# A two-layer perceiver on one core: a third pair of PSUM banks in the last blocks, projections moved between stages, root tables fetched ahead, first loads on a second queue, and products that nothing reads

## The reference

```python
x = x + L0_xattn(ln(x), ctx, mask)   # 16 heads of 16: softmax(q k^T / 4 + (1 - mask) * -10000) v
x = x + L0_attn(ln(x), ...)          # layernorm, causal linear attention over 128 rows, GELU feed-forward
x = x + L0_ffn(ln(x), ...)           # ternary weights, 8-bit activations, silu(gate) * up, down
x = x + L1_xattn(ln(x), ctx)         # as L0, no mask, output projection Wo
x = x + L1_attn(ln(x), ...)          # RWKV recurrence, as scans
x = x + L1_ffn(ln(x), ...)           # ternary w1, depthwise convolution of width 3, silu, ternary w2
```

## Time and profile before

| what | value |
|---|---|
| median of 3 runs | 1111.94 us (1110.3 to 1113.24) |
| the profiled execution | 1110.35 us |
| its span in the trace | 1108.6 us |
| TensorE matmul busy | 1010.3 us, 91% |
| VectorE busy | 737.9 us, 67% |
| ScalarE busy | 685.2 us, 62% |
| GpSimd busy | 437.5 us, 39% |
| mean granted TensorE clock | 0.953 |

### The profile page before, as it was taken

The page is one execution under the profiler, slowest core; times in us unless marked ns, Lnnn a source line. Parts: engine busy times, 40 slices in busy tenths (PEclk is TensorE's granted clock), DMA queues, the critical chain, the costliest instruction groups (busy, mean ns, idle before and its releaser), DMA issues. The chain is left out here.

```text
span 1108.6 us, 30442 instructions
## 1 busy us (share of the span) xinstructions
PE 1010.3 (91%) x12740; PEld 667.8 (60%) x12741; DVE 737.9 (67%) x1723; ACT 685.2 (62%) x963; POOL 437.5 (39%) x388
## 2 busy tenths in 40 slices
PE   7899999999999999887777899999999999999642
PEld 4466666666666666554532566666666666666421
DVE  4888888888888888833357656555656555555455
ACT  3677778777877877776431455555655565655622
POOL 4368888888888888773000000000000000000000
PEclk9999999999999999999985899999999999999965
DMA  7420112110122201130040000111110111000000
GB/s 300 135 69 19 53 66 68 68 56 31 52 69 68 68 22 49 51 151 7 4 180 1 2 24 13 35 35 35 35 35 2 35 35 35 2 2 2 2 1 5
DMA packets 14680, 53.29 MB, mean 48 GB/s; under 512 B 3024, under 2 KB 4816, under 8 KB 13648
## 3 DMA queue, kind: packets, MB, share of 16 engines
q1 hardware_dynamic: 14544, 51.35, 13.3%
HBM read 51.21 MB, written 0.13 MB: 46 GB/s over the span
## 5 line engine op out<-in xcount | busy, mean ns | idle before, releaser
L704 DVE TENSOR_REDUCE tile_max<-ps_max 128x1 f32<-128x448 f32 x448 | 261.0, 620 | 170.4 <-PE ps_max L992 168.1
L701 DVE CUSTOM_DVE_ANT_0 unread<-ps_max,masks 128x448 bf16<-128x448 f32 x432 | 253.6, 621 | 79.0 <-PE ps_max L992 65.6
L393 POOL TENSOR_TENSOR probs<-probs,masks 128x512 f32<-128x512 f32 x196 | 245.3, 1273 | 84.8 <-ACT probs L500 83.7
L509 ACT ACTIVATE probs<-ps_scores 128x1024 f32<-128x1024 f32 x196 | 190.0, 1021 | 96.6 <-PE ps_scores L1015 96.6
L504 ACT ACTIVATE probs<-probs 128x1024 f32<-128x1024 f32 x196 | 207.4, 1058 | 53.3 <-DVE probs L752 46.5
L1015 PE MATMUL ps_scores<-q_pad,k_full 32*128 32x256 f32 x3136 | 233.2, 380 | 0.0
L1031 PE MATMUL ps_out<-probs,values 128*32 128x128 f32 x6272 | 215.9, 278 | 6.1 <-ACT probs L504 5.8
L992 PE MATMUL ps_max<-k_high,q_high 32*128 32x448 bf16 x880 | 199.2, 367 | 17.1 <-DVE tile_max L704 10.1
L1031 PEld LDWEIGHTS ps_out<-probs,values 128*32 128x32 f32 x6272 | 160.5, 110 | 60.7 <-issue 51.1
L1015 PEld LDWEIGHTS ps_scores<-q_pad,k_full 32*128 32x128 f32 x3136 | 193.7, 187 | 0.9
L982 PE MATMUL ps_proj<-ctx_t,wk 128*128 128x448 f32 x368 | 161.8, 562 | 0.0
(11 more groups left out here) (232 smaller groups left out, 678.4 us busy)
## 6 DMA issues: line engine op xcount, KB each, us to landing
ctx_t<-in_ctx_t SPq DMA_DIRECT2D x28, 896.0 KB, 5.3
masks<-in_mask_n SPq DMA_DIRECT2D x14, 448.0 KB, 3.4
masks<-in_mask_t SPq DMA_DIRECT2D x14, 448.0 KB, 3.6
room_w<-in_L_attn_f_w SPq DMA_DIRECT2D x2, 1024.0 KB, 8.8
room_w<-in_L_ffn_w SPq DMA_DIRECT2D x2, 1024.0 KB, 7.5
room_w<-in_L_ffn_w_gate SPq DMA_DIRECT2D x1, 1024.0 KB, 10.6
room_w<-in_L_ffn_w_up SPq DMA_DIRECT2D x1, 1024.0 KB, 13.1
room_w<-in_L_ffn_w_down SPq DMA_DIRECT2D x1, 1024.0 KB, 15.1
```

The costliest lines, as they stand in the source:

```text
L393: nc.gpsimd.tensor_tensor(p, p, three(mask_t[m % 2], TILES)[:, t, :].unsqueeze(1).to_broadcast([P, 4, P]), ALU.add).then_inc(sig("bias_add ...
L509: nc.scalar.activation(prob(T, half), scores_half(half), ACT.Exp).then_inc(sig(f"exp_done{half}"), 1)
L701: ins = v.tensor_tensor_reduce(unread[:, j % 2, :], max_bank(m, j)[:, 0:HALF], mask_n[m % 2][:, HALF * half:HALF * (half + 1)], 1.0, -3e38 ...
L704: ins = v.tensor_reduce(tile_max[:, h, half:half + 1], ps_max[:, j % 2, 0:HALF], AX_X, ALU.max)
```

## The change

- Start: x, `wq` and `bq` of layer 0 are issued from ScalarE's queue; SyncE's begins with `wk`. TensorE computes 5 products of the identity with itself before x is there and 1 behind the first turn, into `ps_out`, which nothing reads. The maxima of block 0 use the `ps_scores` banks first and wait for `q_pad` only from the third on. GpSimd makes `max_change(0)` ahead of the cast `high(1, 1)`.
- Blocks 13 and 27: in odd tiles the first half of the scores goes to `ps_max`. Scores wait for the second half of the tile before and for the first half of two tiles before only. In block 13 VectorE adds the mask to both halves (`bias_last`), second half first, GpSimd adds none, and ScalarE only takes exponentials. No values are made in block 13.
- `BETWEEN` has 15 units: values of 14 take the place of values of 15, and the last key unit of 16 is gone from it. That unit and the values of 15 (`BESIDE`) go between the first maxima of layer 1. These maxima are now taken by pairs of halves, one VectorE instruction over two banks, in three pairs of banks.
- `root_table`: a square root of ones, on ScalarE, behind the last `sums_out` of layer 0 and behind the last GELU; the `between_out` units that stood ahead of `ln_root(1)` and `ln_root(4)` now follow them.
- Tail: 55 products of the identity with `wq[0]` (128x256 each) into `ps_out`, unread: 3, 4, 4, 18, 7, 11 and 8 at seven places.

```diff
@@ helpers
+        def is_last(m):
+            return m % NB == NB - 1
+        def scores_in(T, half):
+            if is_last(T // TILES) and T % TILES % 2 and half == 0:
+                return ps_max[:, :, :]
+            return ps_scores[:, 2 * half:2 * half + 2, :]
+        def pair_bank(i):
+            return (ps_scores[:, 0:2, :], ps_scores[:, 2:4, :], ps_max[:, :, :])[i % 3]
-        BETWEEN += [("v", NB + 1, u) for u in range(PAIRS)] + [("k", NB + 2, j) for j in range(4)]
+        BETWEEN += [("v", NB, u) for u in range(PAIRS)] + [("k", NB + 2, j) for j in range(3)]
+        BESIDE = [("k", NB + 2, 3)] + [("v", NB + 1, u) for u in range(PAIRS)]
+        BESIDE_AT = (1, 4, 7, 10, 13)
-            return m < BLOCKS and m != NB + 1
+            return m < BLOCKS and m not in (NB, NB + 1)
@@ sync
-            sp.dma_start(xs[0][:, :], a["x"]).then_inc(sig("x_loaded"), 16)
-            load_q_weights(0)
@@ gpsimd
-            for c in range(DC):
-                high(1, c)
+            high(1, 0)
...
+                if m == 0:
+                    high(1, 1)
                 for t in range(TILES):
-                    if l == 0:
+                    if l == 0 and not is_last(m):
                         add_bias(m, t)
@@ scalar
+            act.dma_start(xs[0][:, :], a["x"]).then_inc(sig("x_loaded"), 16)
+            act.dma_start(wq[0][:, :, :], a["L0_xattn_Wq"]).then_inc(sig("q_weights0"), 16)
+            act.dma_start(bq[0][:, :], ...).then_inc(sig("q_weights0"), 16)
+            def root_table():
+                act.wait_ge(sig("ones_set"), 1)
+                nc.scalar.activation(stat[:, 30:31], ones[:, 0:1], ACT.Sqrt).then_inc(sig("table_loaded"), 1)
...
-                        if l == 0:
+                        if l == 0 and is_last(m):
+                            exp_in_place(T, 1)
+                            exp_in_place(T, 0)
+                            lent_out(m, t)
+                            projected(m, t)
+                        elif l == 0:
...
-                            exp_scores(T, 0)
-                            exp_scores(T, 1)
+                            exp_scores(T, int(is_last(m)))
+                            exp_scores(T, 1 - int(is_last(m)))
...
-                    between_out(0)
+                    root_table()
                     ln_root(1)
-                    between_out(1)
+                    between_out(0, 1)
...
-                    between_out(8)
+                    act.wait_ge(sig("table_loaded"), 1)
+                    root_table()
                     ln_root(4)
-                    between_out(9)
+                    between_out(8, 9)
@@ vector
+            def pair_maximum(m, i):
...
+                dve.wait_ge(sig("max_ready"), 2 * H * m + 2 * i + 2)
+                two = pair_bank(i)
+                v.tensor_reduce(tile_max[:, i, :], two[:, :, 0:HALF], AX_X, ALU.max).then_inc(sig("max_free"), 2)
+            def bias_last(m, t):
+                T = TILES * m + t
+                dve.wait_ge(sig("bias_t"), 2 * m + 2)
+                need("pv_done", T - 1)
+                for half in (1, 0):
+                    dve.wait_ge(sig("scores_ready"), 2 * T + 1 + half)
+                    v.tensor_tensor(prob(T, half)..., scores_in(T, half)..., mask_t..., ALU.add).then_inc(sig("last_biased"), 1)
@@ tensor
+            def pair_maximum(m, h):
...
+                need("max_free", 2 * H * m + 2 * (h - 2))
+                for half in range(2):
+                    mm(pair_bank(h)[:, half, 0:HALF], ...).then_inc(sig("max_ready"), 1)
@@ tensor, scores
+                spare = is_last(m) and t > 0
+                if m < NB and spare:
+                    pe.wait_ge(sig("max_free"), 2 * H * NB)
+                    pe.wait_ge(sig("last_biased"), 2 * t - 1)
...
-                    pe.wait_ge(sig("exp_done0"), T)
+                elif m > NB or t > 0:
+                    pe.wait_ge(sig("exp_done0"), T - int(spare))
                     pe.wait_ge(sig("exp_done1"), T)
@@ tensor, the rest
+            def idle_products(n):
+                for _ in range(n):
+                    mm(ps_out[:, 0:D], ident[:, :], wq[0][:, 0, :], start=True, stop=True)
             pe.wait_ge(sig("idents"), 3)
+            for _ in range(5):
+                mm(ps_out[:, 0:P], ident[:, :], ident[:, :], start=True, stop=True)
...
+                    for i in range(H):
+                        pair_maximum(NB, i)
+                        if i in BESIDE_AT:
+                            beside_in(BESIDE_AT.index(i))
...
+            idle_products(3)
             pe.wait_ge(sig("ov_ready"), 1)
...
+            idle_products(18)
             pe.wait_ge(sig("wkv_ready"), 1)
```

96 lines of the change are left out of this document (72 added, 24 removed).

## The result

The changed kernel took 1096.19 us (median of 4, 1094.12 to 1096.39) beside 1111.61 of the kernel before in the same job (median of 4): ratio 0.9856, 95% interval 0.9838 to 0.9874. It is faster, but by 1.4% where 2.4% was forecast, and it lies above the range. The profiled execution took 1096.39, its span is 1094.7; before, 1108.6. So 13.9 us of span are to be found, where the forecast had 25.8.

A forecast was written before the change was run, and what follows sets the result against it. TensorE was taken as busy 91% of the span, waiting at the start, block 13, between the layers, block 27 and the tail. Terms summed to 25.8 us off 1110.35, 1084.6; it said 1085, range 1076 to 1094.

The forecast's parts named there:

- Start: Up to the first maxima: full clock earlier, context sooner, GpSimd reordered; −2.5 us, bounds +1 and −4.3.
- the clock comes up during the first key unit: Start: the 6 unread products raise TensorE's clock during that unit, not ahead of it; −2.0 us.
- the 0.4 taken for the three issues less ahead of the context: Start: three issues less on SyncE are about 1.3 us; 0.4 taken, the DMA engines being busy 0.93.
- the start gives nothing: Rival, start: context no earlier, x, wq and bq later by up to 1 us; 1087.5 us, chance 0.15.
- the change leaves blocks 0 to 12 and 14 to 26 as they are: First paragraph: these blocks stay unchanged but for their surroundings; forecast 0 for blocks 0 and 12.
- Block 13: Layer 0's last block: loop S, mask, mask, exponential, W takes 3.1 to 3.2 us per tile; −5.7, bounds −3.5 and −11.4.
- Between the layers: First root −0.5 us; fourth layernorm's root starts at 546.95 and the clock stays up, −3.7, bounds −2.4 and −3.7.
- First maxima of layer 1: Maxima by pairs take 17.4 us and start earlier, −4.2; less 1.7 for VectorE's waits: −2.5, bounds −1 and −4.2.
- Block 14: First tiles: clock falls after the last pair of maxima, returns one tile earlier; −2.0 us, bounds 0 and −7.3.
- Block 27: Last block: spare banks give 2.4 us per tile from tile 3, behind the late sums; −2.9, bounds −2 and −6.
- tiles 3 to 5 give 3 × 0.95: Block 27: each of these three tiles, behind the wait for the late sums, saves 0.95 us.
- Tail: Behind block 27: 55 unread products hold full clock and delay nobody; −6.0 us, bounds −3.5 and −6.0.

The follow-up runs named there:

- loads_back: The change with x, wq and bq issued from SyncE's queue again, ahead of wk: 1091.24 us, ratio 0.9809.
- bq_pause_filled: The change with 7 unread products instead of 1 behind the first turn, in the pause for bq: 1093.53 us, ratio 0.9815.
- start_filled: loads_and_block0 with unread products around layer 1's first maxima and in other pauses, plus 6 ahead of the first key unit: 1078.93 us, ratio 0.9721.
- block0_products: The change with 4 more unread products in the two pauses ahead of the first scores: 1092.04 us, ratio 0.9817.
- bq_back: The change with bq alone issued from SyncE's queue, ahead of wk: ratio 0.983; its profiled execution, 1434.57 us, is left out as slow.
- loads_and_block0: The change with x, wq, bq on SyncE's queue, 4 products ahead of the first scores, late sums' product at block 27's fifth tile: 1085.10 us, ratio 0.9743.
- no_tail_products: The change without the 55 unread products of the tail: 1100.65 us, ratio 0.9878.
- late_at_4: The change with the ones product of the late weights' sums at block 27's fifth tile instead of the third: 1092.39 us, ratio 0.9816.

## Why the prediction was wrong

It gave 1085 and 1076 to 1094; the result is 1096.2. (Its own sum gives 1084.6 for the profiled execution and so 1086.2 for the median; the 1.6 was dropped.) By its own steps:

**Start (−2.5; measured +0.5).** Failed: "the clock comes up during the first key unit", −2.0, and the 0.4 taken for the three issues less ahead of the context, which landed 0.1 to 0.2 earlier. The first maxima started at 19.55, 18.94 before, not "before 17". The products do lift the clock (loads_back), but a pause of 2 us for a load behind them keeps it down; with the pause filled the key unit runs at full clock (bq_pause_filled, start_filled). The rival *the start gives nothing* was right in its mechanism, loads landing later among `wk` and the context, and too mild in its size: it had up to 1 us later, q's projection is 3.2 later (9.11 for the 5.87 of before). The Trainium skill (DMA: Bandwidth & Descriptors, Issuing engines are not separate DMA queues) says that a second issuing engine saves the sequencer's time only. By that rule the start stands still, and the trace goes further: x, first on ScalarE's queue, was there 1.4 us later than as the first on SyncE's, and `bq` took twice as long to land.

**Block 0 (0; +4.0) and block 12 (0; +1.7).** The step that failed is the first paragraph's "the change leaves blocks 0 to 12 and 14 to 26 as they are". The order is unchanged, and a clock that falls in a place where the work has pauses of 1.1 us is not: the two stages were put at nothing without a reason that speaks of their pauses, and the earlier trace rows could not show them, since a fall of 3.4 us in a slice of 27.7 still prints a 9. block0_products shows it for block 0. Block 12 had one fall before too. It has the three pauses of 1.2 us in all 15 profiles (bq_back's left out), and 14 of them have one or two falls there, each 0.5 to 2.1 us behind the end of one of these pauses; the one without a fall, loads_and_block0, needs 33.07, with one fall 34.5 to 34.7, with two 36.1 to 36.2. Blocks 1 to 11 and 15 to 25 have no pause over 0.6 and no fall in any of them. Filling block 12's pauses was not tried, and why the clock falls behind one of them and not behind the next stays open.

**Block 13 (−5.7; −5.9).** Right, and by the loop it gave, S, mask, mask, exponential, W: 3.1 a tile forecast, 3.0 measured from 496.18 to 508.13. Undoing it gives 5.2 back. That the total meets so closely is partly luck: the last scores came 0.9 earlier than walked through, and a fall of the clock at 512.4, behind a pause of 2.08, gave it back (the last `weigh` 1.94 for 1.08; 25.7 in profiles without that fall).

**Between the layers (−0.5 and −3.7; −4.1 by the last down projection).** Right. The root stands at 546.74 where 546.95 was forecast (block 13 ends at 515.0 in either trace, the blocks ahead having lost what it gained, so the two can be compared), and the gate products run at full clock. The load is followed by its root 0.01 later again; the drain of the Trainium skill's page ScalarE: Activation LUTs (What ACT_TABLE_LOAD costs) was not seen.

**First maxima of layer 1 (−2.5; +0.1).** The mechanism was right, a unit at half clock makes VectorE wait once or twice; the term was mis-sized: 1.7 was put for the waits, 4.8 came (2.12 + 2.66). The reductions themselves took 16.5 instead of 17.4, and the first one started 0.5 later than forecast, counted from the down projection. At full clock the same instructions give the forecast and more: in the profile of no_tail_products, with nothing added there, the waits of over 1 us are gone and the way from the end of block 13 to the first scores is 4.8 shorter.

**Block 14 (−2.0; −3.6).** The mechanism was right, the pause after the last pair does bring the clock down again; filling it gives 3.8 more. Two tiles ran at half clock, four before, where the forecast had three.

**Block 27 (−2.9; −1.5).** The pace of the tiles was right, 2.52 for 2.4. What failed is "tiles 3 to 5 give 3 × 0.95": they gave 1.3, since the clock fell at 1031.2, behind the 1.90 of wait for the late sums, and the first two of them took 3.18 and 3.12. Without the wait the block gains 4.7 (late_at_4).

**Tail (−6.0; −5.1).** Right that the products hold the clock and delay nobody: without them 56.3 again. The turns stayed at half clock, behind a wait of 2.02 that the products leave there; the forecast had counted 0.5 for them, which is half of what is missing; the rest is 0.1 or so in each of four other steps. It was not tried with more products.

So the joined change was told right where computing was moved, and wrong where a load was moved and where only the clock moved. Of the 11.9 us that are missing 3.0 are the start, 5.7 are falls of the clock in blocks 0 and 12, 1.1 the stretch between the layers with block 14, 1.4 block 27 and 0.9 the tail; block 13 gave 0.2 more than forecast.

## What to carry to other kernels

Where the clock falls is part of the time, and is no property of an edit: compare stages between two traces before believing a sum, and more than one execution before believing a stage, and count the time at half clock (twice the missing clock times the span; here 0.3 to 0.4 us lost for each). Look for it where TensorE pauses: here most falls stood by pauses of about 1 us and more, also in otherwise dense work (the one at 584 amid pauses of 0.45 between the maxima), and none in the blocks without a pause over 0.6. Unread products paid here in pauses of 0.7 to 9 us with long work behind, where they fitted the pause at full clock and nothing then kept TensorE waiting; ask for each what comes behind it. Loads that the first instructions wait for stay first on the one queue: a second queue beside it made them later here.
